# Logic attention: the value transport rides in the left product, the scores move one step forward, and the last gates and logarithms change places

## The reference, cut to what matters

```python
S1 = einsum('bhnd,bhmd->bhnm', q1, k1) * scale;  S2 = the same of q2, k2
A1, A2 = softmax(S1), softmax(S2)
C_right, C_left = A1 @ A2, A2 @ A1
Cr, Cl = log(C_right + EPS), log(C_left + EPS)
feat = stack([S1, S2, S1^T, S2^T, Cr, Cl])             # 6 maps
hid = gelu(einsum('bhcnm,oc->bhonm', feat, conv1_w) + conv1_b)     # 16 maps
g_and, g_or, g_not, g_chain = sigmoid(einsum(hid, conv2_w) + conv2_b)
Smix = S1 + g_and*S2 + g_or*(logaddexp(S1, S2) - S1) - g_not*0.5*S2 + g_chain*Cr
y_base = softmax(Smix) @ v1
transport = A2 @ v2
y_chain = A1 @ transport
y = y_base + sigmoid(chain_logit) * y_chain;  x + y @ proj_w
```

## Time and profile before

| what | us |
|---|---|
| median of 3 runs | 2507.98 (2504.2 to 2511.65) |
| profiled execution, its own time | 2503.89 |
| its span | 2502.0 |
| the stretch with full periods, about | 155 to 1260 |

### The profile page before, as it was taken

The page is one execution under the profiler, slowest core; times in us unless marked ns, Lnnn a source line. Parts: engine busy times, 40 slices in busy tenths (PEclk is TensorE's granted clock), DMA queues, the critical chain, the costliest instruction groups (busy, mean ns, idle before and its releaser), DMA issues. The chain is left out here.

```text
span 2502.0 us, 55750 instructions
## 1 busy us (share of the span) xinstructions
PE 2187.2 (87%) x22710; PEld 1542.4 (62%) x22710; DVE 1823.9 (73%) x2576; ACT 1671.5 (67%) x2610; POOL 564.3 (23%) x262
## 2 busy tenths in 40 slices
PE   6588999999999999999847868779589999999998
PEld 3454455444544444544335747665479999999998
DVE  3438888898888888888556355662678888888886
ACT  3468888888888888888742243331467777777776
POOL 0124444444444444344200011330000000000000
PEclk9589999999999999999857978999599999999999
DMA  5177677777777777787410000000222222222220
GB/s 172 54 212 223 191 217 212 218 210 204 220 209 222 209 201 221 211 223 203 115 54 1 2 9 2 1 14 11 82 99 72 72 71 71 72 71 71 70 70 24
DMA packets 113320, 305.69 MB, mean 122 GB/s; under 512 B 20479, under 2 KB 57465, under 8 KB 112554
## 3 DMA queue, kind: packets, MB, share of 16 engines
q1 hardware_dynamic: 113066, 302.13, 41.8%
HBM read 169.11 MB, written 80.65 MB: 100 GB/s over the span
## 5 line engine op out<-in xcount | busy, mean ns | idle before, releaser
L722 ACT ACTIVATE la_hid<-ps,la_b 128x904 f32<-128x904 f32 (+1 forms) x480 | 450.4, 988 | 69.2 <-PE ps L577 68.2
L1658 PE MATMUL ps<-ls_xm,ls_w_in_parts 128*128 128x226 f16 x3072 | 467.0, 261 | 12.6 <-DVE ls_xm L1739 8.6
L1666 PE MATMUL ps<-ls_state_parts,ls_w_rec_parts 128*128 128x226 f16 x2976 | 447.0, 258 | 0.0
L1685 ACT ACTIVATE ls_gates<-ps,ls_bias 128x226 f32<-128x226 f32 x768 | 301.0, 445 | 126.1 <-PE ps L1666 125.9
L577 PE MATMUL ps<-la_pairs,la_w 32*64 32x452 f32 x3584 | 309.1, 567 | 45.3 <-ACT la_hid L722 42.5
L1658 PEld LDWEIGHTS ps<-ls_xm,ls_w_in_parts 128*128 128x128 f16 x3072 | 294.5, 97 | 22.0 <-issue 9.2
L1666 PEld LDWEIGHTS ps<-ls_state_parts,ls_w_rec_parts 128*128 128x128 f16 x2976 | 284.7, 96 | 6.0
L590 PE MATMUL ps<-la_hid,la_w 128*32 128x452 f32 x1856 | 247.2, 557 | 1.0 <-ACT la_opened L728 1.0
L551 POOL TENSOR_TENSOR la_P<-la_S,la_top 113x904 f32<-113x904 f32 x64 | 153.3, 2395 | 262.4 <-DVE la_top L825 262.4
L577 PEld LDWEIGHTS ps<-la_pairs,la_w 32*64 32x64 f32 x3584 | 74.1, 130 | 185.6 <-issue 111.6
L728 ACT ACTIVATE la_opened<-ps,la_b 128x904 f32<-128x904 f32 x128 | 129.9, 1015 | 68.5 <-PE ps L590 62.2
(11 more groups left out here) (292 smaller groups left out, 4363.0 us busy)
## 6 DMA issues: line engine op xcount, KB each, us to landing
la_pairs<-la_maps SPq DMA_DIRECT2D x224, 452.0 KB, 6.1
la_gate<-la_opened SPq DMA_DIRECT2D x448, 113.0 KB, 3.8
ls_w_all<-ls_weights SPq DMA_DIRECT2D x32, 904.0 KB, 4.1
la_maps<-la_ST SPq DMA_DIRECT2D x32, 791.0 KB
la_maps<-la_S SPq DMA_DIRECT2D x32, 791.0 KB
ls_m_all<-ls_masks SPq DMA_DIRECT2D x32, 456.0 KB, 3.6
la_maps<-la_Cr SPq DMA_DIRECT2D x32, 395.5 KB
la_maps<-la_Cl SPq DMA_DIRECT2D x32, 395.5 KB
```

Of the source, the lines that this page charges most:

```text
L722: act.activation(hid[:, u % 4, 0:n], ps[:, bank:bank + n, 0:HALF], ACT.Gelu_apprx_tanh, bias=b1[:])\
L1658: mm = pe.matmul(out_j, w_in_parts[:, w, e, j, :], xm[:, t % 2, e, :, x, 0:N], start=((w, x) == PASSES[0]), stop=(t == 0 and (w, x) == PAS ...
L1666: mm = pe.matmul(out_j, w_rec_parts[:, w, e, j, :], state_parts[:, x, e], start=False, stop=((w, x) == PASSES[-1]))
L1685: return act.activation(dst, ps[:, n % 3 * 2 + j // 2, j % 2 * 256:j % 2 * 256 + C], ACT.Tanh if j == 3 else ACT.Sigmoid, bias=bias[:, e, ...
```

## The change

Five edits, all in `logic_attention`.

1. Transport in the left product. P, the tile of softmaxes, gets DK = 16 more columns a head (PV = 129), and DVE writes the values v2 of each head behind A1's columns. The left product A2 @ [A1, v2] then gives C_left and the transport in one matmul of 129 columns a head. The eight matmuls of `transport` go. Six heads (FIRST) lie three to a bank in banks 0 and 1, the last two in bank X. DVE's scaling of the transport and ACT's logarithm are both split into a part of six heads and one of two, and ACT's logarithm waits for DVE's scaling (`T_ready`), since both read the same banks.
2. Last gates first: PE runs `gates(p, 7)` ahead of turning A1.
3. The logarithm of the left product stands ahead of the softplus's.
4. SCORED becomes (0, 2, 4, 6), and ACT copies the turned scores behind units 1 and 5.
5. On DVE `chained` stands ahead of `sums` (the sums of the softmax of image p+2).

```diff
+    PV, FIRST = N + DK, 6
-    SCORED = (1, 3, 4, 6)
+    SCORED = (0, 2, 4, 6)
...
-        V1, V2 = sb("V1", [N, 5, D]), sb("V2", [N, D])
-        P, PT = sb("P", [N, 2, 2, W]), sb("PT", [N, 2, W])
+        V1 = sb("V1", [N, 5, D])
+        P, PT = sb("P", [N, 2, 2, H, PV]), sb("PT", [N, 2, W])
...
+                def left_product(f):
+
+
+                    pe.wait_ge(s["PT2_out"], f + 1)
+                    pe.wait_ge(s["V_ready"], f + 1)
+                    for hd in range(H):
+                        bank, at = (CA + hd // 3, hd % 3) if hd < FIRST else (X, hd - FIRST)
+                        mm = pe.matmul(ps[0:N, bank, at * PV:(at + 1) * PV], PT[:, 1, col(hd)], P[:, f % 2, 0, hd, :],
+                                       start=True, stop=True)
+                        if hd == FIRST - 1:
+                            mm.then_inc(s["prod_made"], 1)
+                    mm.then_inc(s["tail_made"], 1)
...
-                def transport(f):
-                    pe.wait_ge(s["V_ready"], f + 1)
-                    pe.wait_ge(s["PT2_out"], f + 1)
-                    for hd in range(H):
-                        d = slice(hd * DK, (hd + 1) * DK)
-                        mm = pe.matmul(ps[0:N, X, d], PT[:, 1, col(hd)], V2[:, d], start=True, stop=True)
-                    mm.then_inc(s["T_made"], 1)
...
                 def chain(b):
-                    pe.wait_ge(s["T_ready"], b + 1)
+                    pe.wait_ge(s["tail_logged"], b + 1)
...
-                    if ok(f):
-                        turn_softmax(f, 0)
                     if ok(p):
                         gates(p, 7)
                     if ok(f):
+                        turn_softmax(f, 0)
                         turn_softmax(f, 1)
                         values(f)
-                        product(f, 0)
+                        right_product(f)
                     if ok(e):
                         turn_mix(e)
                     if ok(f):
-                        transport(f)
-                        product(f, 1)
+                        left_product(f)
...
+                def log_left(f):
+
+                    act.wait_ge(s["T_ready"], 2 * f + 1)
+                    if f >= 1:
+                        act.wait_ge(ln_saved[(f - 1) % 2], 64 * ((f - 1) // 2 + 1))
+                    x = ps[0:N, CA:CA + 2, 0:3 * PV].rearrange("p k (h n) -> p k h n", n=PV)
+                    act.activation(Cl[:, 0:FIRST * N].rearrange("p (k h n) -> p k h n", k=2, n=N), x[:, :, :, 0:N],
+                                   ACT.Ln, bias=tiny[0:N]).then_inc(s["ln_ready"], 1)
+                    act.wait_ge(s["T_ready"], 2 * f + 2)
+                    x = ps[0:N, X, 0:2 * PV].rearrange("p (h n) -> p h n", n=PV)
+                    act.activation(Cl[:, FIRST * N:W].rearrange("p (h n) -> p h n", n=N), x[:, :, 0:N],
+                                   ACT.Ln, bias=tiny[0:N]).then_inc(s["tail_logged"], 1)
...
-                        if ok(z) and u in (3, 7):
-                            turned_scores(z, u // 7)
+                        if ok(z) and u in (1, 5):
+                            turned_scores(z, u // 5)
...
                     if ok(f):
-                        log_product(f, 0)
+                        log_right(f)
+                    if ok(f):
+                        log_left(f)
                     if ok(p):
                         softplus(p)
-                    if ok(f):
-                        log_product(f, 1)
...
+                    if ok(p + 1):
+                        chained(p + 1)
                     if ok(f):
                         sums(f)
-                    if ok(p + 1):
-                        chained(p + 1)
```

More of the change, by code:

```diff
@@ L549, in _ @@
                             if i == 0:
-                                after(pool, s["prod_made"], 2 * (z - 1))
-                            pool.tensor_tensor(by_head(P[:, z % 2, i]), by_head(S[:, z % 4, i]), per_head(top[:, i]),
+                                after(pool, s["tail_made"], z - 1)
+                            pool.tensor_tensor(P[:, z % 2, i, :, 0:N], by_head(S[:, z % 4, i]), per_head(top[:, i]),
                                                ALU.subtract).then_inc(s["shifted"], 1)
@@ L625, in values, with right_product @@
                     pe.matmul(ps[0:N, X, 0:2 * D], hT[:, f, :], w_v[:], start=True, stop=True).then_inc(s["V_made"], 1)
-                def product(f, i):
-                    pe.wait_ge(s["PT2_out"] if i else s["PT1_out"], f + 1)
+                def right_product(f):
+                    pe.wait_ge(s["PT1_out"], f + 1)
                     for hd in range(H):
-                        mm = pe.matmul(ps[0:N, (CB, CA)[i] + hd // HB, col(hd % HB)], PT[:, i, col(hd)], P[:, f % 2, 1 - i, col(hd)],
+                        mm = pe.matmul(ps[0:N, CB + hd // HB, col(hd % HB)], PT[:, 0, col(hd)], P[:, f % 2, 1, hd, 0:N],
                                        start=True, stop=True)
                     mm.then_inc(s["prod_made"], 1)
+                def left_product(f):
[8 more added lines that the diff above has]
+                    mm.then_inc(s["tail_made"], 1)
                 def turn_mix(e):
@@ L757, in softplus, with log_right @@
                     act.activation(soft[:], soft[:], ACT.Ln, bias=one[0:N]).then_inc(s["soft_logged"], 1)
-                def log_product(f, i):
-                    act.wait_ge(s["prod_made"], 2 * f + i + 1)
-                    if i and f >= 1:
-                        act.wait_ge(ln_saved[(f - 1) % 2], 64 * ((f - 1) // 2 + 1))
-                    to = Cl[:] if i else Cr[:, f % 3]
-                    act.activation(two(to), banks((CB, CA)[i]), ACT.Ln, bias=tiny[0:N]).then_inc(s["ln_ready"], 1)
+                def log_right(f):
+                    act.wait_ge(s["prod_made"], 2 * f + 1)
+                    act.activation(two(Cr[:, f % 3]), banks(CB), ACT.Ln, bias=tiny[0:N]).then_inc(s["ln_ready"], 1)
+                def log_left(f):
+                    act.wait_ge(s["T_ready"], 2 * f + 1)
+                    if f >= 1:
+                        act.wait_ge(ln_saved[(f - 1) % 2], 64 * ((f - 1) // 2 + 1))
+                    x = ps[0:N, CA:CA + 2, 0:3 * PV].rearrange("p k (h n) -> p k h n", n=PV)
[5 more added lines that the diff above has]
+                                   ACT.Ln, bias=tiny[0:N]).then_inc(s["tail_logged"], 1)
                 act.wait_ge(consts_in, ALL_IN)
@@ L874, in values @@
                     dve.tensor_copy(V1[:, f % 5], ps[0:N, X, 0:D])
-                    after(dve, s["T_made"], f)
-                    dve.tensor_copy(V2[:], ps[0:N, X, D:2 * D]).then_inc(s["V_ready"], 1)
+                    after(dve, s["tail_made"], f - 1)
+                    dve.tensor_copy(P[:, f % 2, 0, :, N:PV], ps[0:N, X, D:2 * D].rearrange("p (h d) -> p h d", d=DK)).then_inc(s["V_ready"], 1)
                 def mix_total_of(m):
```

23 lines of the change are left out of this document (15 added, 8 removed).

## The result

The changed kernel takes 2479.2 us in the median (2468.5 to 2495.0, 16 runs) against 2507.6 (2497.9 to 2523.2, 16 runs): a ratio of 0.9892, 95% interval 0.9871 to 0.9913. Forecast were 2470, a range of 2461 to 2495, and 0.88 for faster. The profiled span went from 2502.0 to 2474.9. The gain is 27.1 us of it where my sum said 38.5. It is made up of 5.3 in the ramp, 17.4 in the 29 full periods, nothing in the two periods behind them, and 4.4 from the first gelu of image 31 on, nearly all of it in stages that the change does not touch. At full clock the 29 periods got 38.9 us shorter, more than forecast, and something that I had not priced took 21 us back.

A forecast was written before the change was run, and what follows sets the result against it. No engine was full: a chain changing hands bound the kernel, ACT's work of about 29.2 us plus 5.7 of waits a period. Gains of 34, 0.5 and 4 sum to 38.5, giving 2465.4 profiled, 2470 median; range 2461 to 2495.

The forecast's parts named there:

- my sum: Whole kernel: 34 us from 29 full periods, 0.5 from period 29, 4 from the ramp; 38.5 off the profiled execution.
- the ramp: Before the first convolution, where PE waited 3.53 us for `chained` behind `sums`: 3 to 5 us gained, taken as 4.
- steps through a period: Logic attention's order stepped from measured starts and delays: period falls from 34.87 to about 33.70 us.
- last gates first: End of ACT's units: gates 7 ahead of the turning bring the fourth opening sooner, another 0.9 us a period.
- early scores: Scores starting at about the first gelu, so ACT waits less for them: worth 0.44 us a period.
- split logarithm: Left product's logarithm on ACT: one more instruction costs 0.17 us a period, bounds 0.1 to 0.35.
- cover: End of PE's period: removing transport frees 1.3 to 1.5 us, slack needed by Cl's logarithm and the early scores.
- The first: Rival, 16 in 100: part lost to the next chain, through late `chain`, scaling or gates' DMAs; 2487 or 2485 us.
- DMA mechanism: Fourth opening: gates' DMAs may land at 23.1 or so, ACT asks at 22.83; a 0.5 us wait costs 15 us.
- The half us: Mixing comes half a us sooner without `chained` inside, letting the gates' DMAs go sooner; no wait expected.
- DVE as the bound: Rival, 5 in 100: DVE, working 908/1090 of the stretch, sets the period, so nothing measurable changes; 2503 us.
- a late left product: Rival, 7 in 100: `T_ready` passes beyond 31.9, delaying ACT's left logarithm; at 32.6, 20 us slower, 2528.

The follow-up runs named there:

- E3: Kernel before with only the last gates put ahead of the turning of A1: span 2481.0 us, period 33.86, 29 periods 983.9.
- E9: E5 plus three dummy matmuls between the chain product and the second convolution: 2484.0 us median, ratio 0.9887, periods 34.04.
- E8: Changed kernel with gates, scores and `chained` undone, leaving transport and the order of the logarithms: span 2574.8 us, 35.03 a period at full clock.
- E5: Changed kernel with the scores alone back in their old place, SCORED (1, 3, 4, 6): 2563.1 us median, ratio 1.0217.
- E2: Changed kernel with the eight transport matmuls put back ahead of the left product, result unread: span 2515.2 us, full-clock period 34.53.
- E1: Changed kernel plus two dummy matmuls between the chain product and the first scores: 2468.5 us median, ratio 0.9842.
- E6: E1 with SP issuing the gate DMAs of pair 1 ahead of map loads 4 and 5: 2457.7 us median, ratio 0.9789.
- E7: Changed kernel with `sums` ahead of `chained` on DVE again: span 2550.0 us, 36.55 a period.
- E10: Changed kernel with the softplus's logarithm ahead of the left product's again: span 2515.1 us, 34.15 a period at full clock.
- E4: Kernel before with scores at (0, 2, 4, 6), copies behind units 1 and 5, `chained` ahead of `sums`: span 2521.6 us, 35.33 a period at full clock.
- E11: E6 with SCORED (0, 2, 3, 6), the third scores one step sooner: 2453.1 us median, ratio to the kernel before 0.9765.

## Why the prediction was right, and where it was not

**The steps through a period held.** The period at full clock came out as 33.52 where the sum said 33.70. By parts: last gates first 0.9 forecast, 1.00 measured (E3); early scores 0.44, 0.52 (E9 against the changed kernel); split logarithm -0.17, -0.17 (E8). 29 x 1.34 = 38.9 at full clock instead of the 34 forecast. The ramp gave 5.3 (first gelu of image 0 at 149.93 instead of 155.22) instead of 4, and more than the 3 to 5 I allowed.

**That the time fell into the range is in part luck.** The sum had no term for the clock. The 20.6 us that the falls cost were made up in part by 6 us from periods and ramp that came out better than forecast and by 4.4 from stages behind the attention, and the rest lay within a range made for other losses. The same omission with the scores left in their old place (E5) gives 2563.

**The term that failed is the transport's, "cover".** I priced its removal at nothing but slack, because PE's end of period is not ACT's. Two things were in it. At full clock it is worth 1.01 with the other edits in place (E2); the working had this as the cover that Cl's logarithm and the scores need, and gave no price for it but a us for a us late. And it takes 1.5 us of work out of the one place where PE then has to wait for ACT. The first view I quoted had the granted clock at 0.99 (1.00 over the 29 periods), and I never asked what kept it there. In the changed kernel the falls take 20 us. With transport and the logarithms changed alone they take more than all the edits together give: 1072.5 us for the 29 periods instead of 1010.1 (E8).

**The rivals.** The first named the right size for the wrong reason. A part of the gain was lost, but by the clock, which no rival had. Its DMA mechanism is real and small: 6.1 us of waiting for the gates' landing in the changed kernel, 14.9 in E1, where it is no longer hidden behind falls, and none once SP's order is changed (E6). The half us by which I let these DMAs go sooner was not enough: in the period of the timeline they were the last to come. DVE as the bound and a late left product did not happen: Cl never waited for `T_ready` in the full periods.

**The edits need each other.** At full clock, against the kernel before: gates -1.00, scores with `chained` +0.47, transport with the logarithms +0.17, all together -1.34. The scores can only move up if transport has made room for them, `chained` is ahead of `sums` (E7) and the left logarithm ahead of the softplus's (E10). And transport can only go if something fills the room: the scores in part (E5), or dummy work (E9). Only the last gates' move needs no other.

**What stays open.** That falls follow a gap of PE around the first gelu is shown by E1 and E9, in which filling it removed them. Where the line lies is not: E2 and E4 have the same 0.88 gap as the changed kernel and fewer or shorter falls, E10 has a second gap of 0.86 and no more time at the lower clock, the kernel before and E3 with 0.77 and E9 with 0.56 have none. And the same gap does not always bring one: in E1, E6 and E11 PE waits 1.94 us once, near 214, for Cl's logarithm, and a fall of 3.4 us follows in E6, one of 10.2 in E11, none in E1. In all these kernels the falls in the full periods begin within 4 us behind the first gelu or up to 1.8 ahead of it, and the pattern over the periods repeats regularly (every fifth period in E4, each one in E5), so it depends on more than the gap. Not tried were a filler of half the size in E5's gap, and one of matmuls as narrow as those around it: the filler's have weights of 128x128, so how much of its effect is its width and how much its time is not known.

## What to carry to other kernels

When an edit takes work off PE, ask of every place where PE will now wait whether it is next to another wait, and look at the granted clock over the whole stretch before and after, not at one period. Work that nobody needs, in a gap of 0.9 to 2 us, was worth 17 us of the 29 periods here (11 in the median) and 93 there (79 in the median). And try each edit alone: one of the five gave more in these periods than the five together. And step an order of engines by hand from measured starts: the period came out to 0.2 us in 34, and the next improvement of the order (E11) to less.

## What the runs showed of the hardware that I had not expected

- PE's granted clock fell to 0.50 for 3.4 to 10.2 us at a time although PE was busy 94% of the stretch by the profile (931 of 993 us, its ends modelled). Idle 2.06 us once a period was followed by a fall in nearly every period of E5.
- The falls repeat: with a period of 37.54, one each period (E5); with 35.33, one of 3.4 us every fifth (E4).
- A left product of 129 columns took PE 1.94 against 1.82 for 113 columns, that is 0.12 for 16 columns a head, whereas 16 columns alone had taken 1.67.
- Three matmuls of 128x256 in float32 a period, 1.5 us of 34, held the clock of E9 at 1.00 in all 29 periods, where E5 had 0.87.
